# Attention: the products for the row maxima on all 128 rows of TensorE instead of 32

## The chip, the cores and the metric

The kernel runs on one core of a Trainium2 chip. The metric is device time in microseconds (us) of one execution, here the median of three. The engines are TensorE (PE for its products, PEld for its weight loads), VectorE (DVE), ScalarE (ACT), GpSimd (POOL) and SyncE (SP), which only issues DMAs.

## What is computed

x has 4 batches of 1024 tokens with 128 features. Four blocks follow each other, each on the layer-normalised x and each added to x: causal attention, a mixture of experts, a message block, and the mixture of experts again. Only attention is touched. Cut to what matters (LN is the layer norm of each head's 8 numbers):

```
k, q, v = x@Wk, x@Wq, x@Wv       # 16 heads of 8 numbers
k, q = LN(k), LN(q)
dot = (q . k) / sqrt(8), causal: -inf above the diagonal
attn = softmax(dot)               # over the keys
out = (attn . v) @ Wo + bo
```

## The kernel before, in words

The heads are handled in groups of four (GROUPS = 4 for each batch, 16 groups in all). Each head's 8 numbers are split into a high and a low part and stacked to 32 numbers (STACK), so a group's four heads fill 128 partitions, 32 for each. `qT`, `kT` and `qmT` hold a group's queries, keys, and queries with the row maximum subtracted, [128 partitions, 1024 tokens], each in two buffers (group g uses g % 2).

For each group there are two passes of products:

- The maxima pass (`maxima_unit`, L407 to L417): for query tile qt (128 queries) and keys k0 to k1, a unit makes the products of two heads (a "pair") into the two halves of a PSUM buffer, L413. Each product takes the 32 rows of its head. On the diagonal, two bf16 products of 128 rows add the causal mask, L416. VectorE reduces the unit to two columns of maxima, L743. There are 24 units for each group: 12 of 512 keys a head, and 4 each of 384, 256 and 128. 16 of them have a mask.
- The score pass (`scores`, L423 to L430): again 24 units of two heads, keys by queries, each product on 32 rows (L429). ScalarE takes the exponential into `a_prob` (L561), GpSimd cuts the diagonal (L648), and `weigh` (L432 to L450) multiplies with the values: 128 rows by 32 columns, four heads beside each other, fp32 (L447).

Transposes (L384, 128 rows) turn the stacked queries and keys; ScalarE copies them out of PSUM to `qT`, `kT` and `qmT` (L555), the accumulator to `oT` (L566).

All units share a ring of three PSUM buffers (`pairs`, RINGS = 3) in one order that every engine follows: the generator `sequence` (L293 to L334). While the scores of group g are made ("score", 0 to 23), the steps of group g+1 are put between them: "stack" (two turns, queries first, then keys), 24 "max" units spread evenly over the scores `begin` to 19, "shift" (subtract the maxima) and "turn_shifted". `begin` is 2, or 6 for the last group of a batch. The turns stand behind the scores begin-2 and begin-1. `Units` counts the units; `wait_emptied` waits until a unit's buffer has been read. TensorE executes in the order written, so a wait in front of one product holds everything behind it.

The first group has no scores to hide under: its turns and 24 maxima units run by themselves. In the last group there are no maxima left to make. SyncE has only one job in this phase: 40 DMAs that clear buffers in HBM for the later blocks (L373).

Of the kernel before, what the change touches and what calls it, by code (L numbers as in the profile page):

```python
# [14 lines left out]
P = 128  # L15
# [88 lines left out]
def setup_phase(nc, d, k):  # L104

    with ExitStack() as ctx, ExitStack() as phase:
# [5 lines left out]
        def sem(name):  # L112
# [16 lines left out]
            sem(n) for n in ("below_ones", "below_done", "clear_zero", "rows_counted", "row_doubled"))  # L129
        centre = sem("centre")  # L130
        head_sums = sb("head_sums", [P, 2 * HEADS])
# [27 lines left out]
        @block.gpsimd  # L159
        def _(pool):  # L160
            pool.memset(k["ident"][:, :], 0.0).then_inc(ident_zero, 1)
            pool.memset(k["mask"][:, :], 0.0).then_inc(ident_zero, 1)
            pool.wait_ge(ident_zero, 2)
            pool.affine_select(out=k["ident"][:, :], in_=k["ident"][:, :], compare_op=ALU.not_equal, fill=1.0,
                               base=0, pattern=[[-1, P]], channel_multiplier=1).then_inc(ident_done, 1)

            pool.affine_select(out=k["mask"][:, :], in_=k["mask"][:, :], compare_op=ALU.is_ge, fill=MASKED,
                               base=0, pattern=[[-1, P]], channel_multiplier=1).then_inc(consts_done, 1)
            pool.memset(k["clear_rows"][:, :, :], 0.0).then_inc(clear_zero, 1)
            pool.memset(k["ones"][:, :], 1.0).then_inc(below_ones, 1)  # L170
            pool.memset(k["below"][:, :], 1.0).then_inc(below_ones, 1)
            pool.wait_ge(below_ones, 2)

            pool.affine_select(out=k["below"][:, :], in_=k["below"][:, :], compare_op=ALU.is_ge, fill=0.0,
                               base=-1, pattern=[[1, P]], channel_multiplier=-1).then_inc(below_done, 1)

        @block.vector
        def _(dve):
            dve.memset(ones_row[:, :], 1.0).then_inc(ones_done, 1)
            dve.wait_ge(ident_done, 1)  # L180
            dve.tensor_copy(k["ident16"][:, :], k["ident"][:, :]).then_inc(ident16_done, 1)
# [39 lines left out]
def attention_phase(nc, k):  # L221
# [8 lines left out]
    with ExitStack() as ctx, ExitStack() as phase:  # L230
# [5 lines left out]
        def sem(name):  # L236
# [21 lines left out]
        proj = sb("a_proj", [P, TILES, DIM])  # L258
        steps = sb("a_steps", [P, TILES])
        ones_column = k["ones"][:, 0:1]  # L260

# [6 lines left out]
            sem(n) for n in ("a_squares_ready", "a_rstd_ready", "a_scaled_done", "a_affine_done", "a_v_ready"))  # L268
        unit_full, kept, weighed, o_free = (sem(n) for n in ("a_unit_full", "a_kept", "a_weighed", "a_o_free"))
        unit_free = [sem(f"a_unit_free{i}") for i in range(RINGS)]  # L270
# [22 lines left out]
        def sequence(g, prev, prep, follows):  # L293

            begin, end, made = (6 if g == GROUPS - 1 else 2), 19, 0
            for i in range(SCORE_UNITS):
                yield "score", i
                if follows and i in (begin - 2, begin - 1):
                    yield "stack", i - begin + 2
                if prev and i == 2:  # L300
# [68 lines left out]
        def _(sp):  # L369
            for name in ("f1", "f2"):  # L370
                for rows in k["sent_rows", name]:
                    for n in range(0, HALF_NB, RING):
                        sp.dma_start(rows[n * P:(n + RING) * P, :].rearrange("(n p) e -> p n e", p=P), k["clear_rows"][:, :, :]).then_inc(rows_clear, 16)  # L373
            sp.wait_ge(rows_clear, 16 * 2 * HALVES * (HALF_NB // RING))

        @block.tensor
        def _(pe):
# [25 lines left out]
            def turn_stack(u, nb, g, i):  # L403
                pe.wait_ge(stack_ready, GROUPS * nb + g + 1)
                return turn_tiles(u, heads_of((q_st, k_st)[i], g), range(TILES))

            def maxima_unit(u, g, n, stacks=()):  # L407
                qt, pair, k0, k1, masked, _ = MAXES[n]
                out = by_head(u.next(), k1 - k0)
                u.wait_empty(pe, *stacks)  # L410
                for i in range(2):
                    rows = head_rows(2 * pair + i)
                    mm = pe.matmul(out[:, i, :], qT[g % 2][rows, qt * P:(qt + 1) * P], kT[g % 2][rows, k0:k1], start=True, stop=not masked)  # L413
                if masked:
# [53 lines left out]
            def group(u, b, g, prev, prep, follows, shifted):  # L468
# [4 lines left out]
                for what, n in sequence(g, prev, prep, follows):  # L473
# [5 lines left out]
                    elif what == "max":  # L479
                        maxima_unit(u, ahead, n, stacks if n == 0 else ())  # L480
                    elif what == "turn_shifted":
# [23 lines left out]
            for n in range(len(MAXES)):  # L505
                maxima_unit(u, 0, n, stacks if n == 0 else ())
            shifted = turn_shifted(u, 0, 0)
# [18 lines left out]
        def _(act):  # L526
# [41 lines left out]
            def group(u, b, g, prev, prep, follows, projects=()):  # L568

                G, ahead = GROUPS * b + g, (g + 1) % GROUPS  # L570
                for what, n in sequence(g, prev, prep, follows):
                    if what == "score":
                        weights(u, n)
                    elif what == "stack":
                        empty(u, (qT, kT)[n][ahead % 2])
                    elif what == "turn_shifted":
# [26 lines left out]
            for i in range(2):  # L603
                empty(u, (qT, kT)[i][0])
            u.n += len(MAXES)
# [1378 lines left out]
def hybrid_kernel(nc, d, out):  # L1984
# [8 lines left out]
    with ExitStack() as whole:  # L1993
# [8 lines left out]
        with ExitStack() as attention:  # L2002
            allocate(attention, k, {"ident16": ([P, P], BF16), "mask": ([P, P], BF16),
                                    "w_qkv": ([P, 3 * DIM], F32), "w_o": ([P, DIM], F32),
                                    "ln_rows": ([P, 4 * HD], F32), "bo_rows": ([P, DIM], F32),
                                    "clear_rows": ([P, RING, ROW], F32)})
            setup_phase(nc, d, k)
# [33 lines left out]
```

## Time and profile before

| | |
|---|---|
| three runs | 3357.04, 3361.61, 3369.52 us; median 3361.61 |
| span of the profiled execution | 3276.4 us, first to last instruction |
| what lies around the span | 80.6 to 93.1 us by these runs, 85.2 us against the median (the profiled execution has no separate total) |
| attention, with setup | 0 to about 888 us of the span |
| PE busy over the span | 2931.8 us, 89% |
| mean granted clock of TensorE | 0.891 of full speed |

The page cuts the span in 40 slices of 82 us. A digit is a share in tenths. "PEclk" is the clock that TensorE was granted. Attention takes the first eleven slices.
### The profile page before, as it was taken

What the parts mean: (1) busy time and instruction counts of PE and PEld (TensorE: products, weight loads), DVE (VectorE), ACT (ScalarE), POOL (GpSimd) and SP (SyncE); (2) the same over time, 40 slices, a digit from 0 to 9 for tenths busy, and PEclk for the clock granted to TensorE, in tenths of its full rate; (3) what the DMA queues carried; (4) which work ended last, traced back from release to release, by engine and by line L of the source; (5) the groups of instructions that cost most, each with busy time, mean ns of one, the idle gap of its engine ahead of it and who ended that gap; (6) DMA issues with size and microseconds to landing.
All of it is one profiled execution on the core that took longest, in us unless ns stands there. A gap on an engine that the chain in (4) does not pass through costs nothing. (4 is left out here: it accounts for less than half of the span.)

```text
span 3276.4 us, 55735 instructions
## 1 busy us (share of the span) xinstructions
PE 2931.8 (89%) x18642; PEld 1710.9 (52%) x18643; DVE 1759.5 (54%) x3206; ACT 1418.6 (43%) x2072; POOL 715.3 (22%) x865
## 2 busy tenths in 40 slices
PE   3898888988759995999999999999999999966997
PEld 1333343334348883555555555555555555545886
DVE  3555556555366674455555555554455544546666
ACT  1454455544534443444444444444444444424443
POOL 3031131311256331111111111111111111135632
PEclk7676777766769997999999999999999999976998
DMA  9000000000122215888888888888888888842222
GB/s 160 1 1 1 1 1 1 1 1 1 39 72 65 85 38 125 201 200 195 200 195 196 200 195 199 191 199 195 200 199 190 201 197 200 198 117 74 63 69 79
DMA packets 202915, 388.79 MB, mean 119 GB/s; under 512 B 44561, under 2 KB 117146, under 8 KB 198554
## 3 DMA queue, kind: packets, MB, share of 16 engines
q1 hardware_dynamic: 193562, 367.95, 48.8%
q0 software_dynamic: 9216, 19.02, 1.7%
q8 instruction: 84, 1.38, 0.2%
q14 instruction: 53, 0.43, 0.0%
HBM read 35.23 MB, written 31.75 MB: 20 GB/s over the span
## 5 line engine op out<-in xcount | busy, mean ns | idle before, releaser
L1911 DVE STREAM_TRANSPOSE m_turned<-m_sig 128x1024 f32<-128x1024 f32 x512 | 613.1, 1226 | 595.6 <-ACT m_sig L1824 575.1
L1824 ACT ACTIVATE m_sig<-m_f_ps 128x1024 f32<-128x1024 f32 x512 | 496.4, 1022 | 607.2 <-PE m_f_ps L1696 607.2
L743 DVE TENSOR_REDUCE a_maxima<-a_pair 128x2 f32<-128x1024 f32 (+3 forms) x384 | 354.7, 953 | 304.4 <-PE a_pair L416 240.2
L1709 PE MATMUL m_v_ps<-m_sig,m_tok 128*64 128x512 f32 x2048 | 496.1, 605 | 0.0
L1721 PE MATMUL m_v_ps<-m_sigT,m_tok 128*64 128x256 f32 x4096 | 465.6, 380 | 7.0 <-DMA m_sigT<-m_turned 6.9
L1696 PE MATMUL m_f_ps<-m_swap,m_own 64*128 64x512 f32 x1536 | 442.9, 421 | 11.0 <-DMA m_swap<-m_own 8.8
L1696 PE MATMUL m_f_ps<-m_own,m_swap 64*128 64x512 f32 x1536 | 442.9, 421 | 0.0
L561 ACT ACTIVATE a_prob<-a_pair 128x1024 f32<-128x1024 f32 (+3 forms) x384 | 303.3, 815 | 308.8 <-PE a_pair L429 299.8
L1721 PEld LDWEIGHTS m_v_ps<-m_sigT,m_tok 128*64 128x64 f32 x4096 | 293.8, 138 | 212.4 <-issue 69.1
L1696 PEld LDWEIGHTS m_f_ps<-m_swap,m_own 64*128 64x128 f32 x1536 | 270.9, 186 | 141.1 <-issue 86.0
L1848 POOL TENSOR_TENSOR m_own<-m_uv,m_own 128x1024 fp32r<-128x1024 f32 x64 | 152.0, 2375 | 841.0 <-ACT m_own L1809 841.0
L1696 PEld LDWEIGHTS m_f_ps<-m_own,m_swap 64*128 64x128 f32 x1536 | 270.8, 186 | 3.6
L1709 PEld LDWEIGHTS m_v_ps<-m_sig,m_tok 128*64 128x64 f32 x2048 | 124.4, 136 | 238.8 <-issue 238.8
L429 PE MATMUL a_pair<-a_qmT,a_kT 32*128 32x512 f32 (+3 forms) x768 | 193.5, 544 | 40.2 <-ACT a_prob L561 17.7
L413 PE MATMUL a_pair<-a_kT,a_qT 32*128 32x512 f32 (+3 forms) x768 | 188.4, 549 | 40.7 <-DVE a_maxima L743 17.7
L447 PE MATMUL a_o_acc<-a_prob,a_v 128*32 128x512 f32 (+3 forms) x1536 | 219.8, 692 | 5.3 <-POOL a_prob L648 4.9
L1297 POOL DMA_INDIRECT back_rows<-f_y_rows,f_goes_to x160 | 154.5, 966 | 244.2 <-DVE f_y_rows L1473 236.1
L429 PEld LDWEIGHTS a_pair<-a_qmT,a_kT 32*128 32x128 f32 x768 | 79.7, 224 | 194.3 <-issue 115.2
L1814 ACT COPY m_tok<-m_unit 128x512 f32<-128x512 f32 x128 | 68.8, 589 | 249.4 <-PE m_unit L1680 249.4
L1143 PE MATMUL f_y_ps<-f_w_down,f_innerT 128*128 x1280 | 169.5, 276 | 1.6 <-DVE f_y_rows L1473 1.2
L646 POOL TENSOR_TENSOR a_steps<-ones 128x1 f32<-128x1 f32 x128 | 25.5, 200 | 655.3 <-ACT a_prob L561 655.3
L1920 DVE COPY m_v1T<-m_v_ps 128x256 f32<-128x256 f32 x128 | 54.3, 425 | 193.6 <-PE m_v_ps L1721 193.2
(282 smaller groups left out, 4077.4 us busy)
## 6 DMA issues: line engine op xcount, KB each, us to landing
m_sigT<-m_turned SPq DMA_DIRECT2D x2048, 128.0 KB, 2.4
m_swap<-m_own SPq DMA_DIRECT2D x64, 512.0 KB, 4.4
m_swap<-m_own SPq DMA_DIRECT2D x64, 256.0 KB, 5.0
f_t_rows<-f_sent_rows SPq DMA_DIRECT2D x162, 65.0 KB, 1.8
f_sent_rows<-clear_rows SPq DMA_DIRECT2D x40, 260.0 KB
f_h<-back_rows SPq DMA_DIRECT2D x8, 512.0 KB, 5.0
f_norm_all<-back_rows SPq DMA_DIRECT2D x8, 512.0 KB, 5.6
back_rows<-f_y_rows,f_goes_to POOLq DMA_INDIRECT x160, 2.3
```

The costliest lines, as they stand in the source:

```text
L413: mm = pe.matmul(out[:, i, :], qT[g % 2][rows, qt * P:(qt + 1) * P], kT[g % 2][rows, k0:k1], start=True, stop=not masked)
L429: mm = pe.matmul(out[:, i, :], kT[g % 2][rows, j * P:(j + 1) * P], qmT[g % 2][rows, q0:q1], start=True, stop=True)
L447: mm = pe.matmul(o_acc[h * STACK:(h + 1) * STACK, q0:q1], v1[:, j, g * GROUP + h, :], prob[j % 2][:, h, q0:q1], start=(j == 0), stop=(j == ...
L561: act.activation(prob[j % 2][:, 2 * pair:2 * pair + 2, q0:q1], src, ACT.Exp).then_inc(u.free(), 1)
L743: dve.tensor_reduce(maxima[:, qt, 2 * pair:2 * pair + 2, part], src, AX.X, ALU.max).then_inc(u.free(), 1)
L1143: mm = pe.matmul(y_ps[:, 0:DIM], innerT[p][:, ib * P:(ib + 1) * P], w_down[:, ds(e * INTER + ib * DIM, DIM)], start=(ib == 0), stop=(ib == ...
L1297: pool.indirect_dma_start(back_rows[n // HALF_NB][:, :], bass.IndirectOffsetOnAxis(ap=goes_to[n % UNROLL][:, :], axis=0), y_rows[n % RING] ...
L1696: mm = pe.matmul(f_ps[s][:, cols], tile_of(u[rows, :], j + s * SIDE), v[rows, cols], start=start, stop=stop)
L1709: mm = pe.matmul(v2_ps[h * RANK:(h + 1) * RANK, :], tok[p][:, j + s * SIDE, 0, :], sig[j % 2][s][:, h * HALF:(h + 1) * HALF], start=(j == ...
L1721: mm = pe.matmul(v1_ps[h * RANK:(h + 1) * RANK, g * 2 * P:(g + 1) * 2 * P], tok[p][:, jj, 1, :], sigT[g][:, :, 2 * h:2 * h + 2, jj, :].rea ...
L1824: act.activation(sig[j % 2][s][:, :], f_ps[s][:, :], ACT.Sigmoid).then_inc(sig_ready, 1)
L1911: dve.transpose(turned[g][:, :, q, :, :], sig[j % 2][s][:, :].rearrange("p (t j a) -> p j t a", j=4, a=STACK)).then_inc(turn_ready, 1)
```

## The change

The maxima products take all 128 rows. For this the keys are laid out once more, in a buffer `k_apart` [128 partitions, 4 heads, 1024 tokens]: in the block of head h only the 32 partitions of head h hold keys, the others hold zeros. All 128 rows of `qT` are the other operand, and the zeros remove the other heads. There are two such buffers, zeroed once in the setup, one by GpSimd and one by VectorE (128 x 4096 numbers each). Once `kT` of a group has been copied, SyncE issues four DMAs, one for each head, of 32 partitions x 1024 numbers (128 KB). TensorE waits for them ahead of the first maxima unit of each group. The keys are now turned first and the queries second. `begin` becomes 4 (8 for the last group of a batch): the turns stay where they were and the maxima start two scores later, 24 in 16 scores (12) instead of 18 (14). Scores, mask, weighing and everything else are as before.

```diff
@@ setup, gpsimd
+            pool.memset(k["k_apart0"][:, :, :].bitcast(F32), 0.0).then_inc(apart_zero, 1)
+            pool.wait_ge(apart_zero, 1)
@@ setup, vector
             dve.memset(ones_row[:, :], 1.0).then_inc(ones_done, 1)
+            dve.memset(k["k_apart1"][:, :, :].bitcast(F32), 0.0).then_inc(other_zero, 1)
@@ sequence
-            begin, end, made = (6 if g == GROUPS - 1 else 2), 19, 0
+            begin, end, made = (8 if g == GROUPS - 1 else 4), 19, 0
...
-                if follows and i in (begin - 2, begin - 1):
-                    yield "stack", i - begin + 2
+                if follows and i in (begin - 4, begin - 3):
+                    yield "stack", i - begin + 4
@@ sync, behind the 40 clearing DMAs
+            def spread(u, g):
+                u.wait_emptied(sp, u.n)
+                for h in range(GROUP):
+                    rows = head_rows(h)
+                    sp.dma_start(k_apart[g % 2][rows, h, :].bitcast(F32), kT[g % 2][rows, :].bitcast(F32)).then_inc(k_spread, 16)
...
+                    if what == "stack" and n == 0:
+                        spread(u, (g + 1) % GROUPS)
@@ tensor, turn_stack
-                return turn_tiles(u, heads_of((q_st, k_st)[i], g), range(TILES))
+                return turn_tiles(u, heads_of((k_st, q_st)[i], g), range(TILES))
@@ tensor, maxima_unit
+                if n == 0:
+                    pe.wait_ge(k_spread, 16 * GROUP * (G + 1))
                 for i in range(2):
-                    rows = head_rows(2 * pair + i)
-                    mm = pe.matmul(out[:, i, :], qT[g % 2][rows, qt * P:(qt + 1) * P], kT[g % 2][rows, k0:k1], start=True, stop=not masked)
+                    mm = pe.matmul(out[:, i, :], qT[g % 2][:, qt * P:(qt + 1) * P], k_apart[g % 2][:, 2 * pair + i, k0:k1], start=True, stop=not masked)
@@ scalar
-                        empty(u, (qT, kT)[n][ahead % 2])
+                        empty(u, (kT, qT)[n][ahead % 2])
```

## Rows read from the trace of the kernel before

**Rows 1.** The page: engines, then 40 slices in tenths.
```profile
PE 2931.8 (89%) x18642; PEld 1710.9 (52%) x18643; DVE 1759.5 (54%) x3206; ACT 1418.6 (43%) x2072; POOL 715.3 (22%) x865
PEclk7676777766769997999999999999999999976998
```
**Rows 2.** Windows: start:end, length, busy (count) PE PEld DVE ACT POOL, clock, DMA.
```profile
245.00:296.10 51.10, 47.51 (x260) 20.34 (x256) 25.11 (x36) 22.28 (x30) 6.19 (x16) 0.60 0.00 1
453.40:499.30 45.90, 41.52 (x260) 18.31 (x256) 25.36 (x36) 22.22 (x29) 6.45 (x16) 0.74 0.00 1
99.10:849.50 750.40, 663.36 (x3968) 296.78 (x3968) 417.20 (x631) 372.27 (x474) 145.21 (x262) 0.72 0.00 1
```
**Rows 3.** Waits from 99.1 to 849.5 us: total us, times, longest.
```profile
ACT a_prob L561 <- PE a_pair L429: 296.1, 178, 4.4
DVE a_maxima L743 <- PE a_pair L416: 238.3, 144, 10.6
```
**Rows 4.** Windows: two long stretches, then shorter ones around changes of clock.
```profile
263.00:293.60 30.60, 29.17 (x148) 11.22 (x146) 20.32 (x28) 9.30 (x12) 2.56 (x7) 0.50 0.00 1
177.60:208.30 30.70, 26.97 (x198) 12.97 (x194) 13.20 (x17) 19.25 (x29) 8.35 (x14) 1.00 0.00 1
...
245.30:249.30 4.00, 2.77 (x24) 1.59 (x23) 0.00 (x0) 3.93 (x6) 1.55 (x4) 1.00 0.00 0
219.00:223.00 4.00, 3.87 (x20) 2.41 (x20) 1.54 (x5) 1.18 (x2) 3.84 (x3) 0.50 0.00 0
```
**Rows 5.** Windows of L447 alone (PE, PEld, clock), ahead of two rises.
```profile
211.20:215.20 4.00, 3.01 (x16) 0.60 (x16) 0.51 0.00 0
289.70:293.70 4.00, 2.92 (x16) 0.41 (x16) 0.51 0.00 0
```
**Rows 6.** Timeline of PE at full clock: start us, length, line, operation, shape, count.
```profile
199.78 0.50 PE L429 MATMUL a_pair<-a_qmT,a_kT 32*128 32x512 f32 x2 [0.24 <-ACT a_qmT L555]
200.21 1.09 PE L384 MATMUL a_pair<-ident,a_q_st 128*128 128x128 f32 x8
...
205.28 0.50 PE L429 MATMUL a_pair<-a_qmT,a_kT 32*128 32x512 f32 x2
205.40 0.38 PE L413 MATMUL a_pair<-a_kT,a_qT 32*128 32x256 f32 x2
205.72 0.29 PE L416 MATMUL a_pair<-mask,ident 128*128 128x128 bf16 x2
```
**Rows 7.** Timeline of PE at the lower clock.
```profile
208.29 0.69 PE L413 MATMUL a_pair<-a_kT,a_qT 32*128 32x384 f32 x2
208.91 0.40 PE L416 MATMUL a_pair<-mask,ident 128*128 128x128 bf16 x2
```
**Rows 8.** Timeline of PE in the experts: products of 128 rows by 512.
```profile
1110.40 0.40 PE L1123 MATMUL f_gate<-f_w_hi,f_t_hi 128*128 x1
1110.63 0.39 PE L1124 MATMUL f_gate<-f_w_lo,f_t_hi 128*128 x1
```
**Rows 9.** Groups of instructions from 99.1 to 849.5 us: count | busy, mean ns.
```profile
L743 DVE TENSOR_REDUCE a_maxima<-a_pair 128x2 f32<-128x1024 f32 x180 | 212.5, 1218 | 80.8 <-PE a_pair L413 62.4 <-PE a_pair L416 18.0
L561 ACT ACTIVATE a_prob<-a_pair 128x1024 f32<-128x1024 f32 x180 | 182.5, 1028 | 153.2 <-PE a_pair L429 144.9 <-PE a_pair L413 7.0
```
**Rows 10.** The page's DMA issues: count, KB each, us to landing.
```profile
m_sigT<-m_turned SPq DMA_DIRECT2D x2048, 128.0 KB, 2.4
m_swap<-m_own SPq DMA_DIRECT2D x64, 512.0 KB, 4.4
```
**Rows 11.** Timeline of the first group and the setup.
```profile
12.76 0.17 DVE L184 TENSOR_SCALAR ln_rows<-vec_rows 128x16 f32<-128x16 f32 x1 [10.00 <-PE vec_rows L207]
15.93 3.51 POOL L623 MEMSET a_k_st<- 128x4096 f32 x1 [12.90 <-POOLq L92]
...
68.76 1.01 ACT L555 CAST a_qT<-a_pair 128x1024 fp32r<-128x1024 f32 x1 [18.34 <-PE a_pair L384]
71.62 0.47 PE L413 MATMUL a_pair<-a_kT,a_qT 32*128 32x128 f32 x2 [1.19 <-ACT a_kT L555]
```

More of the change, by code:

```diff
@@ L129, in setup_phase @@
             sem(n) for n in ("below_ones", "below_done", "clear_zero", "rows_counted", "row_doubled"))
-        centre = sem("centre")
+        centre, apart_zero, other_zero = (sem(n) for n in ("centre", "apart_zero", "other_zero"))
         head_sums = sb("head_sums", [P, 2 * HEADS])
@@ L259, in attention_phase @@
         steps = sb("a_steps", [P, TILES])
+        k_apart = [k["k_apart0"], k["k_apart1"]]
         ones_column = k["ones"][:, 0:1]
@@ L268, in attention_phase @@
             sem(n) for n in ("a_squares_ready", "a_rstd_ready", "a_scaled_done", "a_affine_done", "a_v_ready"))
-        unit_full, kept, weighed, o_free = (sem(n) for n in ("a_unit_full", "a_kept", "a_weighed", "a_o_free"))
+        unit_full, kept, weighed, o_free, k_spread = (sem(n) for n in ("a_unit_full", "a_kept", "a_weighed", "a_o_free", "a_k_spread"))
         unit_free = [sem(f"a_unit_free{i}") for i in range(RINGS)]
@@ L373, in _, with group @@
                         sp.dma_start(rows[n * P:(n + RING) * P, :].rearrange("(n p) e -> p n e", p=P), k["clear_rows"][:, :, :]).then_inc(rows_clear, 16)
+            def spread(u, g):
[3 more added lines that the diff above has]
+                    sp.dma_start(k_apart[g % 2][rows, h, :].bitcast(F32), kT[g % 2][rows, :].bitcast(F32)).then_inc(k_spread, 16)
+            def group(u, g, prev, prep, follows):
+                for what, n in sequence(g, prev, prep, follows):
+                    if what in ("score", "stack", "max", "turn_shifted", "turn_out", "turn_tokens", "project_out", "turn_z", "project"):
+                        u.next()
+                    if what == "stack" and n == 0:
+                        spread(u, (g + 1) % GROUPS)
+            u = Units(0, 0)
+            u.n += 2 + 4 + 1
+            spread(u, 0)
+            u.n += 1 + 24 + 1
+            group(u, 0, False, False, True)
+            with sp.Fori(0, BATCH - 1) as b:
+                u = Units(b, UNITS_BEFORE)
+                for g in (1, 2, 3, 0):
+                    group(u, g, True, True, True)
+            u = Units(BATCH - 1, UNITS_BEFORE)
+            for g in (1, 2, 3):
+                group(u, g, True, False, g < GROUPS - 1)
             sp.wait_ge(rows_clear, 16 * 2 * HALVES * (HALF_NB // RING))
@@ L404, in turn_stack, with maxima_unit @@
                 pe.wait_ge(stack_ready, GROUPS * nb + g + 1)
-                return turn_tiles(u, heads_of((q_st, k_st)[i], g), range(TILES))
-            def maxima_unit(u, g, n, stacks=()):
+                return turn_tiles(u, heads_of((k_st, q_st)[i], g), range(TILES))
+            def maxima_unit(u, G, g, n, stacks=()):
                 qt, pair, k0, k1, masked, _ = MAXES[n]
@@ L479, in group @@
                     elif what == "max":
-                        maxima_unit(u, ahead, n, stacks if n == 0 else ())
+                        maxima_unit(u, G + 1, ahead, n, stacks if n == 0 else ())
                     elif what == "turn_shifted":
@@ L505, in _ @@
             for n in range(len(MAXES)):
-                maxima_unit(u, 0, n, stacks if n == 0 else ())
+                maxima_unit(u, 0, 0, n, stacks if n == 0 else ())
             shifted = turn_shifted(u, 0, 0)
@@ L603, in _ @@
             for i in range(2):
-                empty(u, (qT, kT)[i][0])
+                empty(u, (kT, qT)[i][0])
             u.n += len(MAXES)
@@ L2005, in hybrid_kernel @@
                                     "ln_rows": ([P, 4 * HD], F32), "bo_rows": ([P, DIM], F32),
-                                    "clear_rows": ([P, RING, ROW], F32)})
+                                    "clear_rows": ([P, RING, ROW], F32),
+                                    "k_apart0": ([P, GROUP, SEQ], F32R), "k_apart1": ([P, GROUP, SEQ], F32R)})
             setup_phase(nc, d, k)
```

## The prediction

> **What bounds the kernel now.** I read the page first, then the windows of attention, then its waits, then the timeline at single products. On the page PE is busy 89% of the span, yet its clock row shows 6s and 7s in the first eleven slices and mostly 9s later [rows 1]. The change touches only those slices. The 15 groups of heads that carry maxima and scores together run from 99.1 to 849.5 us, cut where ScalarE ends a copy into `qmT`. That is 750.4 us or 50.0 us a group, with PE busy 663 us, DVE 417, ACT 372 and a mean clock of 0.72 [rows 2]. 0.72 means that 2 x 0.28 x 50.0 = 28.0 us of each group ran at the lower level, 56%. ScalarE's longest wait is for score products (296.1 us) and VectorE's for the mask behind the maxima products (238.3 us) [rows 3]. Both wait for PE. So PE's order bounds this phase, and its clock decides how long that order takes.
>
> What a microsecond at the lower clock costs can be read from two groups with the same work (260 products and 256 weight loads each): 51.1 us at 0.60 and 45.9 at 0.74 [rows 2], or 40.9 and 23.9 us at the lower clock. The slope is (51.1 - 45.9)/(40.9 - 23.9) = 0.31. The mean group would take 50.0 - 0.31 x 28.0 = 41.4 us at full clock throughout, and 41.4/(1 - 0.31) = 60 us at the lower one.
>
> **What the clock follows.** From 263.0 to 293.6 us PE is busy 29.17 of 30.6 us and is granted 0.50 all the time; from 177.6 to 208.3 it is busy 26.97 of 30.7 and has 1.00 [rows 4]. Busy time alone doesn't decide. Ahead of two rises stands a weighing, L447, which fills all rows and, by four heads side by side, all columns: 2.9 and 3.0 of the last 4 us [rows 5]. From 219.0 to 223.0, PE is busy 3.87 of 4.0 us with mostly 32-row tiles and stays at 0.50. Ahead of a fall, 245.3 to 249.3, PE is busy 2.77 of 4.0 us and ACT is full (3.93) [rows 4]. I conclude that a tile on 32 rows counts for less than one on 128. The change makes every maxima product four times as tall and runs a pair's two products one behind the other, so the same maxima would hold the clock much better. That is the possible gain. Its price is PE time.
>
> By the Trainium skill, "TensorE: Matmul & The Clock Gate", Part 1, the gate follows how busy the engine has recently been. Read as busy time, that would leave the clock where it is and make this the second rival below; the first pair of windows speaks against that reading.
>
> **The change part by part, for one group.**
>
> *Products in series.* Two 32-row products of a pair start together and share the time of one. With 128 rows they can't. Two 128 x 512 products with new weights start 0.23 us apart at full clock [rows 8], which is little more than one column a cycle at 2.4 GHz. The 24 units hold 12 x 512 + 4 x (384 + 256 + 128) = 9216 columns per head of the pair. The second head adds 9216 columns: 3.9 us at full clock, 7.7 us at the lower.
>
> *Score to maxima.* Now a 32-row tile follows another: at full clock 0.12 us after it where the row groups differ (205.28 to 205.40) [rows 6]. Afterwards this is a change from 32 to 128 rows, as from 199.78 to 200.21: 0.43 us for 512 columns, 0.22 above their stream. At the lower clock the change costs 0.30 above it (208.29 to 208.91 for 384 columns, 0.32 of stream) [rows 6, 7]. There are 16 such places. Bounds: 0 (where a wait covers it) to 0.5 us each, where two units now overlap fully. I take 0.1 more at full clock (+1.6), since most of these places are paced by a full buffer ring, and 0.24 at the lower (+3.8), where PE is full.
>
> *Maxima to mask.* This is such a change now (205.40 to 205.72, 0.21 above 256 columns [rows 6]) and isn't one later: 16 x 0.2 = -3.2 us, or 16 x 0.28 = -4.5 us at the lower clock. Bounds 0 to -4.8. The eight units without a mask lose overlap with their neighbour, 0 to +2 us at the lower clock; I take +1.
>
> By the Trainium skill, "TensorEngine Tiling (Array Packing)", Key Properties, changing the tiling mode drains the engine. The trace agrees, with the 0.22 and 0.30 us just read.
>
> *Sum.* At full clock 3.9 + 1.6 - 3.2 = +2.3 us. There PE isn't full (26.97 of 30.7), so a part hides beside reductions of 1.22 us and exponentials of 1.03 us [rows 4, 9]: I take +1.8, 43.2 us a group. At the lower clock PE is full and nothing hides: 7.7 + 3.8 - 4.5 + 1 = +8, about 67.5 us. One lower-clock microsecond then costs (67.5 - 43.2)/67.5 = 0.36 us.
>
> *Four DMAs a group.* 128 KB lands in 2.4 us, 512 KB in 4.4 [rows 10]; the four of 128 KB move what the one of 512 KB does, and with three more issues I take 4.6 us after `kT`. In between stand the `qT` copy and at least one exponential (2.0 us), then two more scores. The exposed rest is 0 to 2.6 us, and all scores queued behind that first maxima unit wait with it. I take 0.5, since each of the three scores needs a buffer that an exponential of 1.03 us must free. SyncE's queue is otherwise empty here.
>
> *Maxima two scores later.* The two scores no longer have maxima beside them, at a place where ScalarE is full (245.3 to 249.3) [rows 4]; the rest gets denser. 0 to 2 us; I take 0.2, because the same work leaves the denser part.
>
> *Once only.* The two memsets (3.51 us for such a size on POOL) fit under the 10.0 us for which DVE waits in the setup, and under POOL's 12.90 us [rows 11]: 0; at most 3.5 us without that cover. In the first group the keys are copied first and end at 69.8 us (68.76 + 1.01), the DMAs land some 4.6 us later at 74.4 or behind the last clearing DMA, and the first maxima unit, now at 71.6, waits: +3 to +6, I take +5. Its 24 units are paced by VectorE: 0 to +3, taken as 0.
>
> *How much stays at the lower clock.* This is the term that decides, and only bounds are to be had: 56% (no effect) down to about 5%. Of the eight falls between 119 and 304 us, two come at the head of a group like the one at 249.3 [rows 4], with ScalarE full and few or no maxima products, and will stay. In the other six maxima products are running; half might go. That leaves 5 of 8. The lower-clock stretches between also get shorter, since in them the maxima work towards a rise instead of waiting for the next weighing; by a third, say. 28.0 x 5/8 x 2/3 = 11.7 us a group, a quarter of it.
>
> **Total.** 43.2 + 0.36 x 11.7 + 0.5 + 0.2 = 48.1 us, 1.9 less than 50.0. 15 x -1.9 = -28, plus 5 at the start: -23 us. The last group (no maxima) and all behind attention are unchanged. The span becomes 3253 us. These durations come from one execution; 85 us lie between its span and the median, and that stays, so 3361.6 - 23 = 3339, said as 3340. A change under 0.5%, 17 us, can't be told from none here.
>
> **The rivals.**
>
> 1. *The clock stays up almost throughout.* The maxima are spread over 16 of 24 scores and would bridge what the weighings don't. For it: the lower-clock stretches with busy PE. Against: the ACT-bound head of each group. At 8%: 43.2/(1 - 0.36 x 0.08) + 0.7 = 45.2 us, 15 x -4.8 + 5 = -67: 3295 us. Chance 0.20.
> 2. *The clock falls at each head of a group and doesn't come back before a weighing, and the taller products run at 1.2 GHz.* One mechanism, PE time at the lower clock. At 50%: 43.2/(1 - 0.36 x 0.5) + 0.7 = 53.4 us, 15 x 3.4 + 5 = +56: 3418 us. It decides from 33% on, where a group takes 49.7 us and the sum is zero. For it: two scores more without maxima, plus a wait for the DMAs, just where PE is idle already. Against: [rows 4, 5] as read above. Without any effect on the clock (56%) it would be +77. Chance 0.27.
> 3. *The spread keys come late in each group.* 2.6 us instead of 0.5: +31 on the forecast, +8: 3370 us. For it: all four DMAs must land. Against: a ring of three buffers paces the scores between. Chance 0.10.
>
> The forecast has 0.42. That the products are not what the text says, for instance split into more passes, has 0.01.
>
> **How the numbers follow.** The forecast's own range is -50 to +5, with 0.27 of its 0.42 below -17. Faster: 0.27 + 0.19 from the first rival = 0.46. Slower: 0.24 of the second and 0.04 of the third = 0.28. Within 0.5%: 0.26. The range leaves out the far ends of the first two rivals: 3290 to 3415.
>
> **What would show it.** In windows of the same 15 groups: a mean clock of about 0.87 instead of 0.72 (0.95 for the first rival, under 0.8 for the second). Maxima products as 128*128, a pair's starts 0.23 us apart; maxima to mask without the 0.2 us. A wait of the first maxima product for the DMA, about 0.5 us (third rival: over 2). First maxima unit near 76 us. I am wrong if the clock rises to 0.87 and the groups still take 50 us; then PE doesn't bound them and something else does.

## The result: 42.6 us slower, and the profile after

The changed kernel takes 3404.19 us (3398.41 to 3409.99, four runs) against 3361.59 (3357.04 to 3369.52, four runs) for the kernel before on the same chip: a ratio of 1.0134, 95% interval 1.0110 to 1.0158. I had forecast 3340. The time lies inside my range, but on the wrong side of no change.

First the page of the changed kernel: its PE line and its clock row (40 slices, tenths), as [rows 1].

```profile
PE 2973.1 (87%) x18642; PEld 1767.8 (52%) x18643; DVE 1757.5 (52%) x3207; ACT 1418.9 (42%) x2072; POOL 724.7 (21%) x866
PEclk8798877887867997999999999999999999965998
```

The clock rose in the slices of attention, as forecast. The windows show it against [rows 2]: first the same 15 groups of heads, then all that follows attention. Columns as there (length, busy time of PE, PEld, DVE, ACT, POOL, clock, DMA).

```profile
102.90:890.70 787.80, 689.73 (x3968) 343.97 (x3968) 414.94 (x631) 373.01 (x473) 146.16 (x262) 0.83 0.05 11
924.90:3405.60 2480.70, 2222.86 (x14346) 1388.48 (x14346) 1296.18 (x2475) 1012.65 (x1551) 536.56 (x560) 0.94 0.64 151
```

The mean clock is 0.83 instead of 0.72, so 2 x 0.172 x 52.5 = 18 us of a group run at the lower level instead of 28. Still a group takes 787.8/15 = 52.5 us instead of 50.0. Fifteen times 2.5 is 37.4 us, the first group ends 3.8 us later (102.9 against 99.1), and attention ends 40 us later (924.9 against 885.0). That is the result, within what single executions differ by.

The second row needs a warning. The same window of the profile before reads:

```profile
885.00:3276.40 2391.40, 2205.59 (x14346) 1380.02 (x14346) 1298.37 (x2475) 1013.05 (x1551) 534.07 (x560) 0.95 0.66 157
```

The same instructions take 89 us less there. The runs come from different chips. Beside the changed kernel, and on chip 8 later, the unchanged kernel takes 3362 us; on chips 1, 7 and 14 it takes 3267 to 3271. A second trace of the kernel before (e0, chip 1, 3265.19 us) has 2389 us behind attention, the changed kernel and e1 to e4 (chip 8) have 2480 to 2483. The chip of the first trace isn't on record, but its 2391 us put it with the faster ones. So my 85 us "around the span" was mostly this difference: the profiled run of the changed kernel took 3407.34 us with a span of 3405.6, and only 1.7 us lie around it. Of the 93 us between the medians on chips 1 and 8, about 90 lie behind attention, so the attention parts can be compared to within a few us; the two spans can't. All experiments below are compared with the kernel before on their own chip.

The waits from 99 to 891 us (total us, times, longest), as [rows 3], with the new one:

```profile
ACT a_prob L594 <- PE a_pair L462: 337.7, 204, 6.8
DVE a_maxima L776 <- PE a_pair L449: 260.1, 130, 12.7
...
PE a_pair L446 <- DMA k_apart<-a_kT: 16.5, 9, 2.0
PEld a_pair L446 <- DMA k_apart<-a_kT: 13.0, 6, 2.2
```

ScalarE and VectorE wait longer for PE than before (337.7 against 296.1, 260.1 against 238.3), although PE's clock is higher. PE waits 16.5 us for the spread keys, 1.8 us in each of nine groups. The row of PEld is no second wait: its six belong to six of the same nine groups. In the other six groups nothing of the wait is exposed. In three of them PE is held 3.5 us by an exponential that ends after the keys have landed, and in three, the last groups of a batch, nine scores stand ahead of the maxima and PE isn't idle. (I first added the two rows, to 2.0 us in each of 15 groups; the expectations of e1, e2 and e4 go by that.)

The place can be seen in the timeline of PE at the head of one group, at full clock, from the first score:

```profile
205.51 0.50 PE L462 MATMUL a_pair<-a_qmT,a_kT 32*128 32x512 f32 x2 [0.27 <-ACT a_qmT L588]
205.93 1.09 PE L415 MATMUL a_pair<-ident,a_k_st 128*128 128x128 f32 x8
206.96 0.49 PE L462 MATMUL a_pair<-a_qmT,a_kT 32*128 32x512 f32 x2
207.38 1.09 PE L415 MATMUL a_pair<-ident,a_q_st 128*128 128x128 f32 x8
208.40 0.49 PE L462 MATMUL a_pair<-a_qmT,a_kT 32*128 32x512 f32 x2
208.83 0.43 PE L480 MATMUL a_o_acc<-a_prob,a_v 128*32 128x128 f32 x8
209.18 0.50 PE L462 MATMUL a_pair<-a_qmT,a_kT 32*128 32x512 f32 x2
209.96 0.45 PE L462 MATMUL a_pair<-a_qmT,a_kT 32*128 32x384 f32 x2 [0.27 <-ACT a_qT L588]
212.29 0.44 PE L446 MATMUL a_pair<-k_apart,a_qT 128*128 128x128 f32 x2 [1.88 <-DMA k_apart<-a_kT]
212.57 0.28 PE L449 MATMUL a_pair<-mask,ident 128*128 128x128 bf16 x2
```

From the first score to the first maxima product it is 6.8 us. The kernel before, in the same group, also at full clock:

```profile
199.78 0.50 PE L429 MATMUL a_pair<-a_qmT,a_kT 32*128 32x512 f32 x2 [0.24 <-ACT a_qmT L555]
...
204.33 0.33 PE L413 MATMUL a_pair<-a_kT,a_qT 32*128 32x128 f32 x2 [0.78 <-ACT a_kT L555]
```

There it is 4.6 us. PE has little to do in this stretch and VectorE nothing to reduce. I call it the head of a group, counted from the end of the copy into `qmT` to the first maxima product. Its body runs from there to the end of the last reduction, and its tail to the next `qmT` copy's end. Means over the 15 groups, from the records:

| us a group | head | body | tail | sum | at the lower clock |
|---|---|---|---|---|---|
| before | 6.1 | 40.7 | 3.2 | 50.0 | 28.4 |
| changed | 8.4 | 40.8 | 3.3 | 52.5 | 18.1 |

In these means nearly the whole loss is in the head. The body has two scores less and a better clock, and is no shorter. (The traced run of the kernel before took longer than most of its kind; e0 has 6.1, 40.1 and 3.1 us, 25.4 at the lower clock, so against it the body is 0.7 us longer.) Two questions follow: what made the head longer, and why the body doesn't shrink. The means mix three kinds of groups, which e2 below takes apart.

### The profile page after: what moved, and what is told of

Its sections match the earlier page's. It is cut to its first block and busy times, and to the rows that moved or that the text cites. A ratio compares the mean times of both kernels' runs of the same rounds, so it can differ in the third digit from the quotient of the medians.

```text
span 3405.6 us, 55832 instructions
## 1 busy us (share of the span) xinstructions
PE 2973.1 (87%) x18642; PEld 1767.8 (52%) x18643; DVE 1757.5 (52%) x3207; ACT 1418.9 (42%) x2072; POOL 724.7 (21%) x866
## 5 line engine op out<-in xcount | busy, mean ns | idle before, releaser
L446 PE MATMUL a_pair<-k_apart,a_qT 128*128 128x512 f32 (+3 forms) x768 | 266.3, 446 | 75.1 <-DVE a_maxima L776 41.7
L446 PEld LDWEIGHTS a_pair<-k_apart,a_qT 128*128 128x128 f32 x768 | 141.2, 226 | 153.3 <-DVE a_maxima L776 71.6
L480 PE MATMUL a_o_acc<-a_prob,a_v 128*32 128x512 f32 (+3 forms) x1536 | 192.9, 614 | 6.1 <-POOL a_prob L681 5.7
L462 PE MATMUL a_pair<-a_qmT,a_kT 32*128 32x512 f32 (+3 forms) x768 | 174.5, 493 | 19.8 <-issue 4.8
L1176 PEld LDWEIGHTS f_y_ps<-f_w_down,f_innerT 128*128 128x128 f32 x1280 | 155.4, 192 | 10.0 <-issue 10.0
```

The costliest lines, as they stand in the source:

```text
L446: mm = pe.matmul(out[:, i, :], qT[g % 2][:, qt * P:(qt + 1) * P], k_apart[g % 2][:, 2 * pair + i, k0:k1], start=True, stop=not masked)
L462: mm = pe.matmul(out[:, i, :], kT[g % 2][rows, j * P:(j + 1) * P], qmT[g % 2][rows, q0:q1], start=True, stop=True)
L480: mm = pe.matmul(o_acc[h * STACK:(h + 1) * STACK, q0:q1], v1[:, j, g * GROUP + h, :], prob[j % 2][:, h, q0:q1], start=(j == 0), stop=(j == ...
L1176: mm = pe.matmul(y_ps[:, 0:DIM], innerT[p][:, ib * P:(ib + 1) * P], w_down[:, ds(e * INTER + ib * DIM, DIM)], start=(ib == 0), stop=(ib == ...
```

## The experiments

Each kernel ran beside the kernel before on the same chip. Differences are between medians.

### The parts one by one

**e1, the tall products alone.** The kernel before, with one line changed:

```diff
-  pe.matmul(out[:, i, :], qT[g % 2][rows, ...], kT[g % 2][rows, k0:k1], ...)
+  pe.matmul(out[:, i, :], qT[g % 2][:, ...], kT[g % 2][:, k0:k1], ...)
```

> The kernel before, with one edit: the maxima products take all 128 rows of the queries and all 128 rows of the keys as they are, so no spread keys, no DMAs, no wait, and the maxima start where they did. (Leaves out: the four heads are not kept apart, so the maxima subtracted are those of their sum.) My theory now: the change loses by two things, the 2.0 us wait for the spread keys in each group and a clock that rises less than forecast, while the tall products alone are about even. Clock of the 15 groups 0.80 to 0.86, group 49 to 50.5 us, time 3345 to 3370 us. Rival A (the tall products and their serial price lose at any clock): 3385 us or more, group over 51.5 us, clock 0.80 to 0.86. Rival B (the clock follows busy time, not rows): clock stays at 0.72 and a group takes 54 us, about 3420 us.

Measured: 3365.85 against 3362.51 us, ratio 1.0008 (0.9983 to 1.0034). The windows of its 15 groups:

```profile
98.70:831.30 732.60, 653.36 (x3968) 335.73 (x3968) 417.14 (x631) 373.76 (x473) 145.96 (x262) 0.87 0.00 1
```

The clock is 0.87, my forecast to the digit, and the time is the same within the interval. That is above the 0.80 to 0.86 that I expected by then. So the clock's gain and the price of the products cancel, and the +42 come from somewhere else. (This profiled run is at the fast end of its runs, 3353.65 us.)

**e3, half as tall.** The changed kernel, its products on the 64 rows of their pair.

> The changed kernel with each maxima product on the 64 rows of its pair of heads instead of 128 (the rest of the spread keys is zero, so the result is the same). A pair's two products still run one behind the other. Theory that the clock follows how many rows work: clock of the 15 groups between 0.72 and 0.83, about 0.77, group 53.5 to 55 us, time 3415 to 3440 us. Rival (it follows busy time alone): clock 0.83 as with 128 rows, and time 3404 us or less, since neighbours on other rows may overlap.

Measured: 3519.08 against 3362.51, ratio 1.0463 (1.0431 to 1.0496): +157, where the changed kernel has +43. Windows:

```profile
110.30:1007.50 897.20, 805.00 (x3968) 368.76 (x3968) 416.70 (x631) 373.29 (x473) 143.98 (x262) 0.70 0.04 10
```

My theory had the direction right and the size wrong: 3519 us is far above 3415 to 3440. 35.7 of 59.8 us of a group ran at the lower clock, against 18.1 of 52.5 in the changed kernel. Only the rows of the products differ between these two: 17.6 us more at the lower clock go with 7.3 us more a group. 1.4 of them can be laid to the masks (in the records at full clock each of the 16 comes 0.09 us later behind 64-row products), so a microsecond at the lower clock costs 0.34 to 0.41, around my 0.36.

The busy share of PE is 805/897 = 90%, as in e1 (653/733 = 89%) and before (663/750 = 88%). The clock is 0.70, 0.87 and 0.72. The comparison with order and wait held equal is this one against the changed kernel (88%, 0.83) and e4 below (86%, 0.71). With busy time nearly equal, the number of rows makes the difference, and 64 rows don't help. By the Trainium skill, "TensorE: Matmul & The Clock Gate", Part 1, the gate follows how busy the engine has recently been. Read as busy time, the three rows contradict it.

**e4, everything but the tall products.** The changed kernel with 32-row products from `kT`; DMAs, wait and order kept.

> The changed kernel with its DMAs, wait and order, but the maxima products are those of the kernel before (32 rows). My theory: wait 2.0 us a group (30 us) and 5 us at the start, and up to 10 us for the maxima in fewer scores: 3396 to 3410 us, with a clock of 0.68 to 0.72. Rival (the wait is hidden, only the tall products cost): 3360 to 3370 us.

Measured: 3423.12, ratio 1.0187 (1.0163 to 1.0212): +61. So within the changed order the tall products are worth -19 us, and the order with the wait costs 61, more than the 34 to 47 that I expected. The clock is 0.71.

**e5, the order alone.** The kernel before with `begin` at 4 (8), turns left where they were, keys first.

> The kernel before with the changed order alone: keys turned first, both turns where they were, maxima two scores later, 24 units in 16 scores (12) instead of 18 (14). No spread keys, no DMA, products on 32 rows. Theory O (from the second experiment against the first, +23 us): the order costs by itself, since two scores at the head of a group lose their maxima and VectorE's reductions get denser: +15 to +30 us, 3378 to 3392 us, group +1 to +2 us, clock at 0.70 to 0.72. Rival S (it was SyncE's DMAs that cost the 23 us, not the order): within 6 us of the kernel before.

Measured: 3304.94 against 3269.39, ratio 1.0114 (1.0085 to 1.0143): +35.5. Windows:

```profile
99.40:871.60 772.20, 660.18 (x3968) 290.35 (x3968) 412.17 (x631) 371.58 (x474) 143.82 (x262) 0.74 0.00 1
```

The clock is the same as before (0.74 in this chip's own run of the kernel before), the instructions are the same, no DMA is added, and a group takes 51.5 us instead of 49.3. The order costs 2.2 us a group, more than I expected here too. I had taken 0.2 in the prediction.

**e2, the wait out of the way.** The changed kernel with products on all rows of `kT`, DMAs still issued, the wait for them moved to the last maxima unit.

> The changed kernel with its DMAs, its order and its start of the maxima, but the products read the keys as they are on 128 rows, and the wait for the DMAs stands at the last maxima unit, where they have long landed. (Leaves out: heads not kept apart, as before.) My theory: the exposed wait of 2.0 us in each of 15 groups goes, and 3 us at the first: 33 us less than the changed kernel, about 3371 us; group 50.3 us. Rival (TensorE would be idle there anyway, since ScalarE paces the head of a group): within 8 us of the changed kernel, about 3400 us, and the idle time shows as waits for a_prob instead.

Measured: 3388.67, ratio 1.0087 (1.0068 to 1.0106): +26. Against e1 (same products) the order costs +23; against the changed kernel the wait costs 42 - 26 = 16, of which 3.9 at the first group (99.0 against 102.9). That is neither the 33 us of my theory, which counted the wait twice, nor within the 8 us of the rival. By the means its head is hardly shorter than with the wait, 8.3 against 8.4 us, and its body is, 39.8 against 40.8. The records by kind of group show why (us a group: head, whole group, at the lower clock):

| | nine plain groups | three with the next batch's layer norm | three last of a batch |
|---|---|---|---|
| before | 5.0, 48.4, 27.5 | 6.8, 56.1, 26.8 | 8.7, 48.7, 33.0 |
| e1 | 4.8, 47.3, 11.7 | 6.3, 58.0, 19.3 | 9.2, 44.2, 6.8 |
| e2 | 5.7, 50.0, 15.6 | 11.9, 59.8, 20.5 | 12.5, 46.8, 14.8 |
| changed | 7.0, 53.3, 22.2 | 9.9, 57.4, 13.7 | 11.2, 45.5, 10.2 |

The nine plain groups are those in which PE waits for the keys. There the wait makes the head 1.3 us longer and the group 3.2, with 6.6 us more at the lower clock. At my 0.36 a microsecond these are 2.4 us, an estimate, so all that is lost behind the head can be the clock's. That the wait is what lowers it isn't shown. One rival stays: e2's products read real keys on all rows where the changed kernel reads zeros on three quarters, so data and wait change together here. In the other six groups e2 happens to be slower than the changed kernel, at a lower clock, and the means hide the difference of the heads. Against the kernel before, the changed one loses 4.8 us in each plain group, 2.0 in the head and 2.8 behind it.

### What in the order costs

**e8, only the swap of the two turns** (keys first), and **e9, only the later start**, both turns moved with it:

```diff
-            begin, end, made = (6 if g == GROUPS - 1 else 2), 19, 0
+            begin, end, made = (8 if g == GROUPS - 1 else 4), 19, 0
```

This is all of e9's edit. e8 has instead the lines of the change that swap `q_st` with `k_st` and `qT` with `kT`.

> The kernel before, with only the two turns of a group swapped: keys first, queries second. Theory: what the order costs is that two more scores stand ahead of the first maxima unit of a group while nothing gets shorter behind it; the swap itself changes no wait, so within 5 us of the kernel before, and 49.3 us a group. Rival: the swap costs, because the queries' turn now ends last and holds the first maxima product: then this kernel has 20 us or more of the 35.5 us that the whole change of order cost.

Measured: 3268.31 against 3266.51, ratio 1.0000 (0.9986 to 1.0014).

> The kernel before, with begin at 4 (8 in the last group of a batch) and both turns two scores later as well, queries first, so that they stand directly ahead of the maxima as before. Theory (scores ahead of the maxima cost about 1.1 us each in a group): +30 to +35 us against the kernel before, head of a group (copy into qmT to first maxima product) 8.3 us, stretch from first maxima product to last reduction 40 us as before. Rival (the gap between the turns and the maxima, or the swap, is what costs): within 8 us of the kernel before.

Measured: 3307.07 against 3266.51, ratio 1.0114 (1.0097 to 1.0131): +40.5, a little more than expected. Head 8.6 us, body 39.7, tail 3.6. So it is the later start, wherever the turns stand.

**e10, one score earlier.** The kernel before, with:

```diff
-            begin, end, made = (6 if g == GROUPS - 1 else 2), 19, 0
+            begin, end, made = (5 if g == GROUPS - 1 else 1), 19, 0
-                if follows and i in (begin - 2, begin - 1):
-                    yield "stack", i - begin + 2
+                if follows and i == begin - 1:
+                    yield "stack", 0
+                    yield "stack", 1
```

> The kernel before, with begin at 1 (5 in the last group of a batch), both turns directly behind the score ahead of it, so the maxima start one score earlier. Theory: 10 to 17 us faster than the kernel before, head 5.0 us, body 40 us. Rival: the two copies of the turns stand directly behind each other on ScalarE and in the ring of three buffers, TensorE waits there for them, and the maxima start no earlier: 0 to +8 us.

Measured: 3235.03 against 3266.51, ratio 0.9902 (0.9885 to 0.9918): 31.5 us faster, twice what I expected. It beats both kernels. Windows of its groups, and the head of the same group as above:

```profile
99.50:799.30 699.80, 617.26 (x3968) 281.17 (x3968) 418.23 (x631) 374.94 (x473) 145.98 (x262) 0.79 0.00 1
```

```profile
194.25 0.49 PE L430 MATMUL a_pair<-a_qmT,a_kT 32*128 32x512 f32 x2 [0.23 <-ACT a_qmT L556]
194.68 1.09 PE L385 MATMUL a_pair<-ident,a_q_st 128*128 128x128 f32 x8
195.61 1.04 PE L385 MATMUL a_pair<-ident,a_k_st 128*128 128x128 f32 x8
196.57 0.50 PE L430 MATMUL a_pair<-a_qmT,a_kT 32*128 32x512 f32 x2
197.79 0.33 PE L414 MATMUL a_pair<-a_kT,a_qT 32*128 32x128 f32 x2 [0.72 <-ACT a_kT L556]
```

3.5 us from the first score to the first maxima product instead of 4.6. A group takes 46.7 us instead of 49.3 in e0 (head 4.9 instead of 6.1, body 38.7 instead of 40.1), and the clock rises from 0.74 to 0.79 with the same 32-row products. That is 40 us in 15 groups; 8 of them are lost again behind attention (2398 us in this trace, 2389 in e0).

**e11, the same early start with the tall products of e1.**

> Products of the maxima on all 128 rows without spread keys (all four heads of a group are added up, so the maxima are those of the sum and not of a head), and begin at 1 (5) as in the kernel with the early start. Theory: 10 to 20 us faster than the same products with begin at 2, which stood 3 us above the kernel before: so -7 to -17 us against the kernel before, clock 0.87. Rival (body bound by the serial products): +3 us as with begin at 2.

Measured: 3259.36 against 3266.51, ratio 0.9973 (0.9950 to 0.9996): -7, at the edge of what I expected, and 24 us more than e10. Windows:

```profile
98.90:843.60 744.70, 677.53 (x3968) 342.83 (x3968) 419.42 (x631) 376.37 (x474) 145.96 (x262) 0.84 0.00 1
```

PE is busy 677.5 us instead of 617.3 at a better clock (0.84 against 0.79). The tall products cost +3 us at the old start and +24 at the early one. The maxima aren't denser here (24 in 19 scores instead of 18), and 16.4 us of a group ran at the lower clock against 12.3 in e1; but the profiled run is the slowest of six (3272.72 us), and why the early start helps them so little isn't shown. Still, even if the keys were spread for nothing, this change would lose to e10.

**e12, the delay taken out of the changed kernel.** `begin` back at 2 (6); DMAs, wait and tall products stay.

> The changed kernel with begin back at 2 (6 in the last group of a batch), its turns, DMAs and 128-row products kept. Theory: the spread keys land about 6 us behind the copy of the keys' turn begins, so the head of a group is held just as long, now by the wait instead of by two scores: within 10 us of the changed kernel, head 7.5 to 8.5 us, wait of PE for the DMA near 3.5 us a group instead of 2. Rival (the two scores themselves cost, and the three buffers hide the transfer): 20 to 33 us faster than the changed kernel.

Measured: 3312.82 against 3271.21, ratio 1.0127 (1.0094 to 1.0160): +41.6, where the changed kernel has +42.6. The head of the same group:

```profile
208.59 0.50 PE L462 MATMUL a_pair<-a_qmT,a_kT 32*128 32x512 f32 x2 [0.24 <-ACT a_qmT L588]
...
215.38 0.44 PE L446 MATMUL a_pair<-k_apart,a_qT 128*128 128x128 f32 x2 [3.03 <-DMA k_apart<-a_kT]
```

6.8 us again, and 7.0 in the mean of the nine plain groups in both kernels (over all 15 it is 8.0 against 8.4, with a body of 41.6 against 40.8). In the waits from 99 to 891 us, where the changed kernel has 16.5 us in nine groups, it now reads:

```profile
PE a_pair L446 <- DMA k_apart<-a_kT: 40.4, 15, 3.4
```

So `begin` = 4 takes 24 us off PE's wait and costs 23 by itself (e2 less e1). It buys nothing, because it fills with two scores a stretch that the spread keys take anyway. The tile view of `k_apart` in the changed kernel (duration ns min/median/max), and SyncE's issues in the timeline, show this chain:

```profile
L383 SPq DMA_DIRECT2D k_apart<-a_kT x60: 507/590/598, 106.8 to 846.1; - x60
...
DMA to landing us min/median/max: 2.2/2.3/2.5
```

```profile
207.06 1.01 ACT L588 CAST a_kT<-a_pair 128x1024 fp32r<-128x1024 f32 x1
```

```profile
208.10 2.41 SPq L383 DMA_DIRECT2D k_apart<-a_kT  x4
```

The copy of the keys ends at 208.07, four issues of 0.59 us in one queue take until 210.5, and the last transfer lands 2.3 us after its issue began (209.9 + 2.3 = 212.2). PE starts at 212.29. The copy to the first product takes 4.2 us. In the kernel before, only the second turn's copy stands there, and PE waits 0.78 us for it. By the Trainium skill, "DMA: Bandwidth & Descriptors", Anatomy of one DMA, a transfer has a fixed part of about 2.0 us whatever its size (measured there on GpSimd's path). The 2.2 to 2.5 us here, on SyncE's, agree. Fewer issues, or issues from two queues, would shorten the other part of this chain; no run tried that.

### The other end

**e6**, the kernel before with `end` = 20 instead of 19; **e7**, e1 with the same; **e14**, `end` = 18; **e13**, e10 with `end` = 18.

> The kernel before with the maxima spread up to score 20 instead of 19, so 24 units in 19 scores (15), and the shift one score later. If it is the density of the maxima that costs (theory O), one score more gives back half of what two scores fewer take: -6 to -12 us. If it is the head of the group without maxima that costs, this changes nothing: within 4 us. A rival: the subtraction comes one score nearer to its turn at score 21, and TensorE waits for it, +10 us or more.

> The first experiment (tall products on the keys as they are, heads not kept apart) with the maxima spread up to score 20. Same theories: density -6 to -12 us against the 3366 us of the first; head alone: no difference. Clock 0.86 to 0.90.

> The kernel before, with the maxima ending behind score 18 instead of 19. Theory (maxima and the chain behind them, subtraction and its turn, set the end of a group; scores left over behind them hide nothing): 10 to 30 us faster, opposite to the 30 us that one score later cost. Rival (at 19 the chain is already covered, and 24 maxima units in one score less crowd TensorE): 0 to +15 us.

> The kernel with the early start (begin 1), with the maxima ending behind score 18 as well. Theory: both gains add up, 40 to 55 us faster than the kernel before. Rival (a group is bound by TensorE's time once the head is short): no more than the 31 us of the early start alone.

| | edit | difference to before, us | ratio, 95% interval |
|---|---|---|---|
| e6 | end 20 | +30 | 1.0103 (1.0067 to 1.0139) |
| e7 | tall, end 20 | +9 | 1.0023 (1.0008 to 1.0038) |
| e14 | end 18 | +9 | 1.0024 (1.0006 to 1.0042) |
| e13 | begin 1, end 18 | +3 | 1.0009 (0.9992 to 1.0026) |

No run gained time. In e14 and e13 that is what the rivals said. In e6 the last one holds: the subtraction comes one score nearer to its turn, and TensorE waits for it. From 99 to 860 us the waits of PE show, for e6 and then for the kernel before (e0):

```profile
PE a_pair L384 <- DVE a_q_st L753: 15.3, 15, 1.4
PE a_pair L384 <- DVE a_q_st L753: 0.7, 3, 0.2
```

That is about half of the 30 us. The body grows too, from 40.1 to 40.7 us, although it has more room. So e6 isn't a clean test of density, but it gives density no support. With `end` at 18, the tail grows from 3.1 to 4.6 us (e14) and 4.5 (e13): scores are left over behind the maxima. e13 also loses what e10 gained in the body (40.3 against 38.7 us) and in the clock (0.73 against 0.79), with the same short head of 4.9 us. So begin and end aren't alike, and a short head alone doesn't raise the clock. Of the four combinations of begin 1 or 2 with end 18 or 19, begin 1 and end 19 is the best, by 31 us or more.

### Why the body doesn't shrink

For this I grouped the stretches between the starts of two reductions following each other, in the records, by whether an exponential starts between them:

| | nothing between | one exponential between |
|---|---|---|
| kernel before (its run beside e5) | 114 of 1.16 us | 216 of 1.81 us |
| e9, two scores later | 144 of 1.15 us | 189 of 1.87 us |
| e10, one score earlier | 100 of 1.17 us | 230 of 1.65 us |
| changed | 135 of 0.97 us | 207 of 2.07 us |

Stretches with two or more exponentials between (3 to 15 a run) are left out, and both clocks are mixed. Two maxima units behind each other take about a reduction's time (1.22 us for the widest); a score between them adds only some 0.65. In the head, a score stands alone and lasts as long as an exponential and more: two scores add 2.5 us to it (e9, 6.1 to 8.6; 1.5 in the nine plain groups, 3.2 and 4.7 in the other kinds). By these means a score costs about 1.25 us there and some 0.65 in the body, and e9's remaining 1.87s are longer as well. The rule that a score is cheaper among maxima fits e9, e5 and e10 in sign, but it is argued from these stretches and not tested by a run of its own. Its size falls short: 0.6 us a score would give +18 us for e9, measured are 40.

## Why the prediction was wrong, step by step

I forecast -23 us and got +43, 66 us off. The runs split this into three. The tall products alone were to bring (43.2 + 0.36 x 11.7 - 50.0) x 15 = -39 us and brought +3 (e1): 42. The later start was to cost 3 and cost 23 (e2 less e1): 20. The wait with the start was to cost 12.5 and cost 16 (changed less e2): 4. The first miss took the gain away, the second made a loss of it.

**The price of the tall products at full clock, +2.3 us, taken as +1.8.** This step failed, and it is the largest miss. Two figures show it. First, *products in series*: I counted 0.23 us from a pair's first product to its second, as in [rows 8]. Behind a score or an idle stretch it is 0.34 us. A pair that lasts 0.74 us shows it, and four products in a row behind a score:

```profile
226.00 0.74 PE L446 MATMUL a_pair<-k_apart,a_qT 128*128 128x512 f32 x2 [0.35 <-DVE a_maxima L776]
274.39 1.20 PE L446 MATMUL a_pair<-k_apart,a_qT 128*128 128x512 f32 x4
```

0.74 less a product's 0.40 leaves 0.34. In the records the four start 0.339, 0.234 and 0.235 us apart: the first step is dear, those behind it have the 0.23 of [rows 8]. Of 152 pairs of 512 at full clock, 36 follow another maxima product straight on, with a median of 0.235; behind a mask it is 0.315 to 0.335, behind a score 0.34. Three in four pay 0.1 us, some 2 us a group. At the lower clock a pair behind a score is 0.59 us apart. Second, *the whole*: PE's busy time times its clock, an estimate of its work in full-clock time, is 650 x 0.74 = 481 us for the 15 groups of e0 and 653 x 0.87 = 568 in e1, so 5.8 us more a group instead of 2.3. The changed kernel (690 x 0.83 = 572) against e4 (682 x 0.71 = 484) gives 5.9. The 3.5 us too few make 52 in 15 groups, enough for the miss of 42; how much of them is hidden no run shows. At the mask the gain was a little smaller than forecast: at full clock the stretch from a unit's first product to its mask goes from 0.26 to 0.28 us for 128 columns and from 0.33 to 0.575 for 512, with both products in series now.

**"Maxima two scores later: 0 to 2 us; I take 0.2, because the same work leaves the denser part."** This step failed too, and it turned an even result into a loss. It cost 1.5 us a group (e2 less e1), 2.2 (e5) or 2.7 (e9), the last two beyond its upper bound. The work did leave the dense part, but the body hardly shrank for it, while in the head it stands alone. The bound should have come from the head itself: two exponentials of 1.03 us [rows 9] and their exchange with PE, 2.5 us in e9, with nothing given back.

**DMA wait, 0.5 us (bounds 0 to 2.6).** PE's exposed wait is 16.5 us, 1.1 a group in the mean and 1.8 where it shows, and never over 2.0. So it lies between my figure and the third rival; in time the wait cost +16 us in all (e2 against changed), with the start. I had the landing 4.6 us after `kT` nearly right (4.2), but counted the scores between by their number: they need 2.3 us (208.07 to the last one's end at 210.41), not 4. That the wait lowers the clock in the same groups wasn't in the sum.

**Start, +5 us.** Measured +3.8: the first maxima unit runs at 75.62 (I said near 76). The memsets cost nothing that shows.

**How much stays at the lower clock, 11.7 us.** Right for the products by themselves: 12.3 in e1. The route to it, 5/8 and a third, was a guess, so this is in part luck. In the changed kernel it is 18.1, most in the groups where PE waits (22.2). By my slope of 0.36 these 6.4 us are 2.3 of the 4.4 us by which a group is longer than forecast. The first rival (clock nearly full) didn't happen; the second (50% at the lower clock) neither: 34% is just at its point of decision (33%).

**What the clock gives back.** I wrote that I'd be wrong if the clock rose to 0.87 and a group still took 50 us, since then PE wouldn't bound it. e1 has 0.87 and 48.8 us a group (e0 on another chip 49.3), and the time of the kernel before within 0.3%. But that sign was badly chosen: PE is busy 653 us in e1 and 650 in e0, so its work grew as the clock rose, and this can't tell whether PE sets the pace. e3 against the changed kernel gives 0.34 to 0.41 us for each at the lower clock, so the slope of 0.36 has support.

## What to carry to other kernels

When a step is delayed so that a transfer can hide, price the place it leaves: work moved out of a dense part saves only what it cost there, and ahead of the dense part it stands alone. Check such a delay by taking it out: where the time stays the same, the delay bought nothing, and the chain behind the wait (copy, issues, landing) is the cost. Take a product's price from a place with the same neighbours, not from a stream of its own kind. A mean over unlike groups can hide where the time goes. Before paying for a better clock, try the order of the work; here a start one score earlier gave 31 us and the tall products none.

## What the runs showed of the hardware

- In runs of the same order and the same wait, TensorE's granted clock was 0.71 with maxima products on 32 rows (e4, PE busy 86%), 0.70 on 64 (e3, 90%) and 0.83 on 128 (changed, 88%). In the old order it was 0.72 on 32 rows and 0.87 on 128 (e1).
- The same program takes 3267 to 3271 us on chips 1, 7 and 14 and 3362 us on chip 8. In the traces of this case the blocks behind attention take 2389 to 2398 us on the chips of the first kind and 2480 to 2483 us on the other, whichever kernel ran; the mean DMA rate in that stretch is 157 GB/s in the first trace and 151 in the changed kernel's. Why, these runs don't show.
- At full clock, the second of two 128 x 512 products with new weights starts 0.235 us after the first where another such product runs straight ahead, and 0.34 us where a 32-row product or an idle stretch does (medians over the changed kernel's records).
